# Loads in order of need, expert biases as one product, value copies on GpSimd, and new instruction orders in a two-half transformer and expert kernel

## What is computed

```python
# block L0: ada gives shift, scale and gain from cond, for attention and for the MLP
xm = expmap0(layer_norm(logmap0(x)) * (1 + sc_msa) + sh_msa)
q, k, v = (to_heads(plin(xm, w, b)) for w, b in ...)      # plin: expmap0(logmap0(x) @ w + b)
out_h = expmap0(softmax(logmap0(q) @ logmap0(k).T / sqrt(8)) @ logmap0(v))   # 16 heads of 8
x = mobius_add(residual, expmap0(g_msa * logmap0(plin(from_heads(out_h), w_o, b_o))))
ff = plin(plin(expmap0(layer_norm(logmap0(x)) * (1 + sc_mlp) + sh_mlp), w_f1, b_f1), w_f2, b_f2)
x = x0 + mobius_add(x, expmap0(g_mlp * logmap0(ff)))
# block L1: experts 0 to 3 weighed by a gate per sequence (top 2 of 4), expert 4 (shared) unweighed
gate = softmax((means_of_x @ gate_w + gate_b) * (1 + scale) + shift)
out = sum_e w[e] * mask[e] * (gelu(x @ ew1[e] + eb1[e]) @ ew2[e] + eb2[e])
out = x + out + gelu(x @ sw1 + sb1) @ sw2 + sb2
```

## Time and profile before

| | |
|---|---|
| median of 3 runs | 189.19 us (187.07 to 191.94) |
| the profiled execution | 187.8 us, of which the span of the core is 185.8 us |
| PE busy | 123.6 us, 67% |
| DVE busy | 99.5 us, 54% |
| ACT busy | 89.3 us, 48% |
| POOL busy | 40.9 us, 22% |
| chain that ended last | PE 54%, DVE 19%, ACT 17%, DMA 5% |

### The profile page before, as it was taken

The page is one execution under the profiler, slowest core; times in us unless marked ns, Lnnn a source line. Parts: engine busy times, 40 slices in busy tenths (PEclk is TensorE's granted clock), DMA queues, the critical chain, the costliest instruction groups (busy, mean ns, idle before and its releaser), DMA issues.

```text
span 185.8 us, 3219 instructions
## 1 busy us (share of the span) xinstructions
PE 123.6 (67%) x1176; PEld 105.8 (57%) x1176; DVE 99.5 (54%) x406; ACT 89.3 (48%) x234; POOL 40.9 (22%) x47
## 2 busy tenths in 40 slices
PE   0064994439651917910218079999999999999974
PEld 0043763438550806800115059799899898899963
DVE  5734487976528764385687734319496350220321
ACT  0433343952857664156496481329734772523500
POOL 7000006807200000000100008982310005940000
PEclk9999997555975596855555855999999999999999
DMA  5990199300000000000000000000000002000002
GB/s 172 373 188 8 41 213 366 127 2 4 4 4 0 0 0 0 4 2 0 0 0 0 0 0 5 0 0 2 4 0 0 0 4 56 0 0 4 0 0 58
DMA packets 8207, 7.61 MB, mean 41 GB/s; under 512 B 2000, under 2 KB 6512, under 8 KB 8192
## 3 DMA queue, kind: packets, MB, share of 16 engines
q1 hardware_dynamic: 7728, 6.86, 13.2%
q10 hardware_dynamic: 464, 0.54, 0.9%
HBM read 6.84 MB, written 0.56 MB: 40 GB/s over the span
## 4 chain that ended last, share of the span: by engine, by line
PE 54%; DVE 19%; ACT 17%; DMA 5%; issue 3%; ACTq 1%; DVEq 0%
PE bank L1318 20%; PE bank L1302 5%; PE bank L1303 5%; PE bank L1304 5%; DMA prob<-w_ada 5%; PE bank L1156 4%; ACT qk L911 3%; PE bank L1168 2%; PE bank L1237 2%; PE bank L1224 2%; DVE heads L420 2%; PE bank L1186 2%; PE bank L1260 2%; PE bank L1288 2%; ACT vblk L877 1%
## 5 line engine op out<-in xcount | busy, mean ns | idle before, releaser
L1318 PE MATMUL bank<-wdn,probT 128*128 128x128 f32 x192 | 24.1, 287 | 1.7 <-DVE xn L669 1.3
L961 ACT ACTIVATE probT<-bank,col 128x512 f32<-128x512 f32 x24 | 15.9, 688 | 18.4 <-PE bank L1304 18.3
L1318 PEld LDWEIGHTS bank<-wdn,probT 128*128 128x128 f32 x192 | 23.6, 203 | 2.1 <-issue 1.9
L1302 PE MATMUL bank<-x3hi,whi 128*128 128x512 f32 x40 | 18.0, 449 | 6.7 <-ACT probT L961 6.7
L669 DVE SCALAR_TENSOR_TENSOR xn<-bank,wtok,xn 128x128 f32<-128x128 f32 x32 | 9.0, 344 | 22.7 <-PE bank L1318 22.7
L1156 PE MATMUL bank<-cst,xn 128*128 128x128 f32 x24 | 5.9, 396 | 16.6 <-DVE xn L556 10.3
L1303 PE MATMUL bank<-x3hi,wlo 128*128 128x512 f32 x40 | 16.6, 415 | 0.0
L1304 PE MATMUL bank<-x3lo,whi 128*128 128x512 f32 x40 | 16.6, 414 | 0.0
L961 ACT ACTIVATE prob<-bank,col 128x512 f32<-128x512 f32 x16 | 10.8, 688 | 10.0 <-PE bank L1304 10.0
L1318 PEld LDWEIGHTS bank<-wdn,prob 128*128 128x128 f32 x128 | 14.8, 192 | 0.2
L1318 PE MATMUL bank<-wdn,prob 128*128 128x128 f32 x128 | 14.9, 275 | 0.0
(11 more groups left out here) (201 smaller groups left out, 274.6 us busy)
## 6 DMA issues: line engine op xcount, KB each, us to landing
wdn<-w_down SPq DMA_DIRECT2D x5, 256.0 KB, 7.3
wraw<-w_up SPq DMA_DIRECT2D x5, 256.0 KB, 6.7
gain<-gain_dram SPq DMA_DIRECT2D x4, 256.0 KB, 5.1
row<-rows SPq DMA_DIRECT2D x1, 774.0 KB, 8.3
wf<-w_f SPq DMA_DIRECT2D x1, 514.0 KB, 10.5
xin<-x SPq DMA_DIRECT2D x2, 256.0 KB, 3.7
xres<-x SPq DMA_DIRECT2D x8, 64.0 KB, 6.4
out<-xn SPq DMA_DIRECT2D x4, 128.0 KB, 1.9
```

Of the source, the lines that this page charges most:

```text
L961: act(hT[e % 2][:, g, c, :], bk(g, (e * FC + c) % 3)[:, :], ACT.Gelu_apprx_tanh, bias=col[:, K_EB1 + e * FC + c:K_EB1 + e * FC + c + 1]).t ...
L1302: mm(z, hi[:, c * P:(c + 1) * P], xhi, start=True, stop=False)
L1318: last = mm(d, hT[e % 2][:, g, c, t * P:(t + 1) * P], wdn[e][:, c, :], start=c == 0, stop=c == FC - 1)
```

## The change

**Loads.** The second half's tokens are loaded from ScalarE's queue, and the first half's from SyncE's. On SyncE's queue the q, k, v weights come second, the broadcast row of biases is loaded in two pieces and without the expert biases (908 columns instead of 1548), the first up weight follows, then the small copies `xsq`, the other up weights, and after them the output and MLP weights and `xres`. On ScalarE's queue `cond` (in `col`) and the `ada` weight come before the constants.

**Expert biases.** The token weights are also made with experts in the rows (`token_rows`, one product of 16 x 5 by 16 x 512 per half, and one VectorE multiplication by the mask). In the shared expert's `down` each output tile then begins with a product of these rows and the five biases (K = 5), eight more products in all. `biases` and `accumulate_biases` are gone.

**GpSimd** copies v into blocks for both halves (`place_v`), takes the reciprocal roots of the second half's first branch (`root_squares(1, 0)`) and the gate's exponential as a power of e (`gate_exp`), and no longer makes biases or additions for `mobius`.

**VectorE and ScalarE.** Head sums are taken tile by tile. q and k are scaled separately. ScalarE expands the last two tiles of q, from another PSUM bank. `mobius` of the MLP makes all four of its intermediate tiles on VectorE. Tables for gelu are loaded explicitly.

**Orders.** The first half takes the experts in the order 0, shared, 1, 2, 3. Up chunks and halves of down are single steps, with tables for their banks, and all lists are written anew.

```diff
+        BANKS = [3, 1, 2, 0]
+        OB = [2, 3]
+
+        SEQ = [[0, E, 1, 2, 3], [0, 1, 2, 3, E]]
+        UP_BANKS = [[0, 1, 2, 0] + [2, 0] + [1, 2, 0] * 5, [0, 1, 2] * 7]
+        DOWN_BANKS = [[[1, 1]] + [[3, 3]] * E, [[3, 3]] * E + [[3, 0]]]
...
-            for g in range(NG):
-                sp.dma_start(xin[:, T(g), :], x[T(g)].rearrange("t p d -> p t d")).then_inc(x_in[g], 16)
-            sp.dma_start(row[:], rows.broadcast_to([P, R_END])).then_inc(s["rows_in"], 16)
+            sp.dma_start(xin[:, T(0), :], x[T(0)].rearrange("t p d -> p t d")).then_inc(x_in[0], 16)
             sp.dma_start(wqkv[:], w_qkv).then_inc(s["wqkv_in"], 16)
+
+            def load_rows(a, b):
+                sp.dma_start(row[:, a:b], rows[:, a:b].broadcast_to([P, b - a])).then_inc(s["rows_in"], 16)
+
+            def load_up(e):
+                sp.dma_start(wraw[:, e, :], w_up[e]).then_inc(up_in[e], 16)
+
+            def load_down(e):
+                sp.dma_start(wdn[e], w_down[e].rearrange("p (c d) -> p c d", c=FC)).then_inc(down_in[e], 16)
+
+            load_rows(R_QKV, R_BO)
+            load_rows(R_BO, R_END)
+            load_up(0)
+            sp.wait_ge(ln_vals[0], nth(LN_VALS, "mean"))
+            for t in range(TG):
+                for b in range(BT):
...
+            for e in SEQ[0][1:]:
+                load_up(e)
             sp.dma_start(wo[:], w_o).then_inc(s["wmlp_in"], 16)
             sp.dma_start(wf[:], w_f).then_inc(s["wmlp_in"], 16)
```

In the functions (VectorE, ScalarE and TensorE):

```diff
+            def head_sum(g, i):
+
+                v.wait_ge(s["qsq_ready"][g], i + 1)
+                n = 3 * H
+                step(nc_v.tensor_reduce(heads[:, g, 0, i * n:(i + 1) * n],
+                                        qsq[:, g, i * 3 * D:(i + 1) * 3 * D].rearrange("p (h d) -> p h d", d=HD), X, ALU.add))
...
+            def clamp_qk(g, j):
+
                 v.wait_ge(s["c_ready"][g], 1)
-                c4 = hh(3)[:, 0:n_hd].rearrange("p (t h) -> p t h", t=TG)[:, :, 0:2 * H]
-                nc_v.tensor_tensor(qk[:, T(g), :].rearrange("p t (h d) -> p t h d", d=HD),
-                                   qkv[:, T(g), 0:2 * D].rearrange("p t (h d) -> p t h d", d=HD),
-                                   c4.unsqueeze(3).broadcast_to([P, TG, 2 * H, HD]), ALU.mult).then_inc(s["qk_ready"][g], 1)
+                c = heads[:, g, 3, 0:n_hd].rearrange("p (t h) -> p t h", t=TG)[:, :, j * H:(j + 1) * H]
+                nc_v.tensor_tensor(qk[:, T(g), j * D:(j + 1) * D].rearrange("p t (h d) -> p t h d", d=HD),
+                                   qkv[:, T(g), j * D:(j + 1) * D].rearrange("p t (h d) -> p t h d", d=HD),
+                                   c.unsqueeze(3).broadcast_to([P, TG, H, HD]), ALU.mult).then_inc(s["qk_ready"][g], 1)
...
+            def token_rows(g):
+
+                v.wait_ge(s["gate_mm"][g], nth(GATES, "rows"))
+                v.wait_ge(s["sels_in"], 16)
+                nc_v.tensor_tensor(wtT[:, g, :], bk(g, 3)[0:E + 1, :], sel[0:E + 1, S_WM:S_WM + GT],
+                                   ALU.mult).then_inc(s["wtT_ready"][g], 1)
...
             mobius(0, 1, x1, x3)
+            branch_out(1, 0, "ap_mm", R_BO, xres)
+            stage_squares(1, 0)
+            gate_inputs(0)
+            branch_norm_late(1, 0)
             x3_low(0)
-            branch_out(1, 0, "ap_mm", R_BO, xres)
...
+            def expand_q(g):
+                a.wait_ge(s["trans_mm"][g], nth(TRANS, "qT"))
+                for h in range(HG):
+                    act(qexp[:, g, TG // 2 * BT:, h, :], bk(g, 2)[:, GT // 2:].rearrange("p (r s) -> p r s", s=S), ACT.Copy,
+                        scale=cst[:, C_HM + h:C_HM + h + 1]).then_inc(s["qexp_late"][g], 1)
...
+            a.dma_start(xin[:, T(1), :], x[T(1)].rearrange("t p d -> p t d")).then_inc(x_in[1], 16)
+            a.dma_start(col[:], cols).then_inc(s["cols_in"], 16)
+            a.dma_start(wada, w_ada).then_inc(s["wada_in"], 16)
             a.dma_start(cst[:], consts).then_inc(s["consts_in"], 16)
-            a.dma_start(col[:], cols).then_inc(s["consts_in"], 16)
-            a.dma_start(wada, w_ada).then_inc(s["wada_in"], 16)
             a.dma_start(sel[:], sels).then_inc(s["sels_in"], 16)
-            a.wait_ge(s["consts_in"], 32)
 
```

```diff
+            def token_rows(g):
+                pe.wait_ge(s["wtok_ready"][g], 1)
+                mm(bk(g, 3)[0:E + 1, :], gw[:, g, :], sel[:, S_SEL:S_SEL + GT], start=True, stop=True) \
+                    .then_inc(s["gate_mm"][g], 1)
...
                 lo, hi, xlo, xhi = wlo[:, e, :], whi[:, e, :], x3lo[:, g, :], x3hi[:, g, :]
                 for c in range(first, end):
-                    k = e * FC + c
-                    if k >= 3:
-                        pe.wait_ge(s["moe_h"][g], k - 2)
-                    z = bk(g, k % 3)[:, :]
+                    n = k * FC + c
+                    b = UP_BANKS[g][n]
+                    before = [m for m in range(n) if UP_BANKS[g][m] == b]
+                    if before:
+                        pe.wait_ge(s["moe_h"][g], before[-1] + 1)
...
+                banks = DOWN_BANKS[g][k]
+                if 3 in banks:
+                    pe.wait_ge(s["wtT_ready"][g], 1)
+                    if k and 3 in DOWN_BANKS[g][k - 1]:
+                        pe.wait_ge(s["moe_acc"][g], k)
+                for t in range(first, end):
+                    i = 2 * t // TG
+                    a = t * D if banks[i] else (t - TG // 2) * D
+                    d = bk(g, banks[i])[:, a:a + D]
                     if e == E:
-                        d = bk(g, LAST[t // 2])[:, t % 2 * D:(t % 2 + 1) * D]
+                        mm(d, wtT[:, g, t * P:(t + 1) * P], sel[0:E + 1, S_B2:S_B2 + D], start=True, stop=False)
```

More of the change, by code:

```diff
@@ L171, in cond_resid_kernel @@
         xres_in = [sem(f"xres_in{g}") for g in range(NG)]
-        w_in = [sem(f"w_in{e}") for e in range(E + 1)]
+        up_in = [sem(f"up_in{e}") for e in range(E + 1)]
+        down_in = [sem(f"down_in{e}") for e in range(E + 1)]
         TRANS = "xnT0 qT kT ainT xnT1 x3T".split()
-        VALS = ["head out tok n0 beta0 h n1 beta1 logit".split(), "head out tok n0 beta0 y h sq n1 beta1 logit".split()]
+        VALS = ["head out tok n0 beta0 h n1 beta1".split(), "head out tok sq0 n0 beta0 y h sq1 n1 beta1".split()]
         LN_VALS = "mean clip var shift".split()
-        FUNCS = "y0 head out tok a0 th0 y1 h a1 th1 gexp".split()
+        FUNCS = "y0 head out tok a0 th0 y1 h a1 th1".split()
         LN_FUNCS = "norm log rstd".split()
-        GATES = "logit token".split()
+        GATES = "logit token rows".split()
         def nth(names, name):
@@ L253, in _ @@
                     .then_inc(s["gain_in"], 16)
-            for e in range(E + 1):
-                load_up(e)
-            for e in range(1, E + 1):
+            for e in SEQ[0]:
                 load_down(e)
@@ L1346, in _ @@
             norm_rows(0, 1)
+            feed_forward(0)
             quadratic(0)
[L1348 removed]
             transpose_x3(0)
+            up(0, 0, 0, 1)
+            up(0, 0, 1, 2)
             gate(0)
[L1351 to L1352 removed]
+            up(0, 0, 2, 3)
+            up(0, 0, 3, 4)
+            up(0, 1, 0, 1)
+            xn_transposed(1, 1)
+            up(0, 1, 1, 2)
+            down(0, 0, 0, 2)
             token_weights(0)
[L1354 removed]
@@ L1366, in _ @@
+            down(0, 1, 2, 4)
+            up(0, 2, 3, 4)
+            up(0, 3, 0, 1)
+            up(0, 3, 1, 2)
+            up(0, 3, 2, 3)
+            down(0, 2, 0, 2)
+            down(0, 2, 2, 4)
+            up(0, 3, 3, 4)
+            up(0, 4, 0, 1)
+            up(0, 4, 1, 2)
             transpose_x3(1)
-            down(0, 3)
-            up(1, 0)
+            down(0, 3, 0, 2)
+            up(1, 0, 0, 1)
+            up(0, 4, 2, 3)
+            up(1, 0, 1, 2)
             gate(1)
-            down(0, 4)
@@ new lines, in _ @@
+            up(1, 1, 3, 4)
+            down(1, 0, 0, 2)
+            down(1, 0, 2, 4)
+            up(1, 2, 0, 1)
+            up(1, 2, 1, 2)
+            up(1, 2, 2, 3)
+            down(1, 1, 0, 2)
+            down(1, 1, 2, 4)
+            up(1, 2, 3, 4)
+            up(1, 3, 0, 1)
+            up(1, 3, 1, 2)
+            up(1, 3, 2, 3)
+            down(1, 2, 0, 2)
+            down(1, 2, 2, 4)
+            up(1, 3, 3, 4)
+            up(1, 4, 0, 1)
+            up(1, 4, 1, 2)
+            down(1, 3, 0, 2)
@@ L1383 @@
+            down(1, 3, 2, 4)
+            up(1, 4, 2, 3)
+            up(1, 4, 3, 4)
+            down(0, 4, 2, 4)
+            down(1, 4, 0, 2)
+            down(1, 4, 2, 4)
 _OUT = (B, S, D)
```

498 lines of the change are left out of this document (263 added, 235 removed).

## The result

The changed kernel takes 193.51 us as a median of 4 runs (192.92 to 193.83), the kernel before 189.25 on the same chip: a ratio of 1.026 with a 95% interval of 1.017 to 1.035. So it is slower, by 1.7 to 3.5% here; 186.5 was forecast, and the range ended at 190.0. In a second comparison it was 1.036 (1.027 to 1.045). Medians in this document are over all executions of a kernel, while ratios with an interval leave out those more than 1.5% above its fastest, the profiled executions of *no bias products*, *no rows* and *combined* among them. The profiled execution is 192.92 us with a span of 190.8; forecast were 185.2 and 183.2.

What follows compares the result with a forecast made beforehand. It took a chain of short steps across engines, then TensorE in the expert stage, as bounds. TensorE resuming at 103.4 plus 77.1 of work gave 180.5, plus 2.7 and 2.0 made 185.2 us profiled, 186.5 median; range 182.5 to 190.0.

Steps and rivals of the forecast that it cites:

- the restart: Expert stage: TensorE resumes after its wait for the third gelu, forecast at 103.4, 10.3 us after the first up product.
- eight bias products: Expert stage, shared expert's down: added products priced at 0.22 us each, +1.8 us together.
- one chunk less: Expert stage: one more up chunk is done before TensorE resumes, -1.5 us, priced at 1.2 GHz.
- Rival (c): Expert stage: TensorE's clock rises late and the second half's x3 is late; 191.2 us profiled, 192.6 median; chance 0.08.
- Token rows: Expert stage: two added TensorE products of 512 columns with the short gaps of such steps, +2.4 us.
- the wait at the end: End of the expert stage: TensorE's wait for accumulate to free the bank goes, covered by another down, -1.3 us.
- the finer weave: Expert stage: waits from interleaving smaller steps on TensorE, +0.8 us, an estimate with bounds 0 and 3.
- rival (d): Expert stage: the half microsecond of margin turns into waits of some 2 us; 187.2 profiled, 188.6 median; chance 0.09.
- the exposed 2.6 us: Front, VectorE: logarithm to the start of normalise, hidden before, now stands behind the ada step, 2.6 us.
- rival (b): Front: ada weight still lands near 10.2, logarithm exposed, normalise at 15.7; 188.0 profiled, 189.3 median; chance 0.09.
- the heads: From normalise to the first exponentials: 1.1 us more gained, bounds 0.4 and 2.0, exponentials at 38.5 instead of 39.92.
- The attention: From the first exponentials to copy_ainT(0): ScalarE reaches it another 1.4 us earlier, at 50.9 instead of 53.73.

Runs made afterwards that it cites:

- no bias products: The changed kernel without the eight bias products in the shared expert's down, token-rows steps kept: 187.87 us, 0.998 of the kernel before.
- no rows: The changed kernel without the eight bias products and without both token-rows steps: 185.42 us, 0.984 of the kernel before.
- combined: The changed kernel with ada step and first up weight late, biases on GpSimd behind the second half's token weights: 182.98 us; again 183.25 us, 0.982.
- full rows: The changed kernel with each of the eight bias products replaced by a product of 128 rows instead of 5: 190.66 us, 1.007 of the kernel before.
- the run on row norms: The changed kernel with the second half's first row norms on TensorE ahead of that half's projections: 192.96 us, 1.023 of the kernel before.
- up weight late: The changed kernel with the ada step behind the logarithm again and the first up weight asked for behind the small copies: 190.76 us.

## Why the prediction was wrong

The profiled end came 7.7 us later than forecast: 1.3 at the restart and 6.3 in the work behind it, against 77.1.

*The step that failed* is "eight bias products of 3.58/16 = 0.22 each (+1.8)". They cost 4.8 (no bias products), and full rows shows why: 0.22 is the price of a product like its neighbours. I had taken the duration from the nearest row by size of output, and not asked whether the rows match; the forecast had no bound on this term at all. That is 3.0 us of the 6.3. The falls below are 3.4 and the rows 0.3 less than priced. The clock rose 1.2 us sooner than before, worth 0.6. And one chunk less was put down at its length at 1.2 GHz, 1.5; if the rise comes at a fixed distance behind the restart, as the sum also assumed, other work moves under the lower clock and only 0.75 is won. So the terms give 3.0 + 3.4 - 0.3 - 0.6 + 0.75 = 6.3.

*The clock.* The condition "if the clock again rises some 7.6 us after the restart" was met and more: it rose 6.0 us after it (before, 7.2 by the clock's record; the 7.6 was read from wider stretches). What I didn't allow for was that it may fall again under unbroken work: 3.4 us in the changed kernel, both times. Rival (c) had the clock rise late and the second half's x3 late, neither of which happened, so that its 192.6 lies near the 193.5 measured is luck. I gave all cases of the clock 0.08. Whether the bias part made the falls likelier stays open: of eight profiled executions with the token rows seven had them (for 1.7 or 3.4 us) and one had none; of the four without rows and without a wait for the gate three had one and one had none; the kernel before had none in its one. Two orders meant to remove the first fall didn't. The second fall was seen only with the token rows or behind the wait for the gate.

*Terms that were right.* Token rows 2.4, measured 2.1. The chunk done earlier, taken at full clock (-0.7), the wait at the end (-1.3) and the finer weave (+0.8) sum to -1.2, and the combined kernel has 1.2 us less at full clock than before; the three are shown only in sum. TensorE waited only 0.47 us in the weave (at 140.7), so rival (d) didn't happen. From the first up product to the restart 10.1 us, forecast 10.3. The restart ahead of the transposes and no wait before the last down are there.

*The front.* The weight landed at 8.66, inside my bounds, not at 7.8. Behind it the 2.87 and the exposed 2.6 us held (undoing the order gave 2.6 back), but the first operation of the logarithm took 0.9 more because GpSimd's split had been moved beside it, and the 0.4 that I took off for an earlier start of the queues had no ground: the ada weight was issued at 1.84, before at 1.76. So `normalise` came at 14.96 instead of 12.9. This nearly was rival (b) by another road. The rule of the Trainium skill cited there holds so far as 0.26 MB taken away moved the start of the ada products by some 0.5 us. From `normalise` to the exponentials the heads gained 1.2, forecast 1.1; the reason I gave, that the norms hold it, was wrong by the run on row norms. The attention gained 0.6 instead of 1.4, and I have no experiment on why. x3 was at 88.6 instead of 86.6. The prediction named as a sign of being wrong that the front's moments come less than 2 us earlier than before: the exponentials came 0.55 later, `copy_ainT` 0.1 earlier and x3 1.3 earlier, so the sign was there. What made the restart early all the same lies behind x3: 6.0 us to the first up product (7.3 before, 6.5 forecast) and 10.1 from there (10.9 before).

What is left of the change, with the biases behind the gate on GpSimd and the two moves in the front taken back, is the combined kernel: 183.25 us against 187.91. So the change held a gain, and the biases on TensorE, the order of the ada step and the falls of the clock hid it.

## What to carry to other kernels

Price an added product by a row with the same number of rows and the same neighbours; here a bias product of 5 rows inside a stream of products of 128 cost 0.61 us, nearly three times the 0.22 of a full one, and GpSimd made the same biases for nothing once it did so while VectorE had no chain of small steps. When a step is moved on one engine, look at what the others do in that microsecond: here a split on GpSimd that the new loads moved into the first microseconds cost 0.9 us on the critical path. When the clock moves between executions, compare the work at full clock and the moments ahead of it, and not one total: here an execution without a fall had paid for it in the MLP branch. And keep one order for what is sure to be late: a step that waits for a load goes behind the work that doesn't need it.

## What the runs showed of the hardware

- A product with 5 rows between products of 128 rows: 0.41 us, and the four behind it 1.09 in place of 0.89, at 2.4 GHz. The weight load is then not ahead of its product; between products of 128 rows it is, by 0.11 us.
- A VectorE operation of 0.15 to 0.22 us on SBUF that met a running GpSimd operation on two SBUF inputs ended with it, after up to 1.24 us; a reduction kept its 0.14, and the ada step, which reads PSUM, its 0.73.
- TensorE's clock fell to 1.2 GHz with the engine busy without a gap, starting at 113 to 116 and at 154 to 155, for a loss of 1.7 or 3.4 us, in some executions of one kernel and not in others; without the fall where the thin products started 1.4 to 1.6 us behind the rise, with it at 0.5 to 0.8. In two executions of the combined kernel the MLP branch had 2.4 GHz for 3.4 us in one and 1.2 GHz throughout in the other. The same eight products of that branch took 1.05 us in the changed kernel and 1.87 with the up weight late. That is larger than most of the gains this change was after.
